# A two-path Mamba-2 stack with experts on one Trainium2 core: the next pass's constants and weight products taken later in a block, and the kernel's own constants built in four stages

## What is computed

```python
def mamba2(x, Win, conv_w, conv_b, dt_bias, A_log, D, gnorm, Wout):
    zxbcdt = x @ Win                                   # 64 -> 296
    z, xBC, dt = split(zxbcdt)                         # 128, 160, 8
    xBC = silu(conv_b + causal_conv4(xBC, conv_w))
    xs, B, C = split(xBC)                              # 128, 16, 16
    dt = softplus(dt + dt_bias)
    dA = exp(dt * -exp(A_log))
    # h_t = dA_t * h_{t-1} + xdt_t B_t ;  y_t = h_t C_t
    y = scan(dA, xs * dt, B, C) + D * xs
    return rmsnorm(y * silu(z), gnorm) @ Wout

for i in range(6):
    x = x + mamba2(rmsnorm(x, t_norm[i]), t_...[i])    # along time
    x = x + mamba2(rmsnorm(x, b_norm[i]), b_...[i])    # along bands
t = x_in + x
out = t + experts(layernorm(t))                        # 16 experts, top 2
```

## Time and profile before

| what | us |
|---|---|
| median of 3 runs | 1553.57 |
| lowest and highest run | 1553.42, 1564.56 |
| the profiled execution | 1553.12 |
| span of that execution | 1551.4 |
| busy: PE, DVE, ACT, POOL | 1220.9, 909.3, 720.8, 276.1 |

### The profile page before, as it was taken

One profiled execution on the slowest core, in us unless ns is written; L12 is line 12 of the kernel. 1 busy time (PEld: TensorE's weight loads), 2 busy tenths in 40 slices (PEclk: granted clock), 3 DMA queues, 4 the chain that ended last, 5 costly groups with the idle time before them and its releaser, 6 DMA issues. The chain is left out here.

```text
span 1551.4 us, 47280 instructions
## 1 busy us (share of the span) xinstructions
PE 1220.9 (79%) x20280; PEld 635.6 (41%) x20280; DVE 909.3 (59%) x1667; ACT 720.8 (46%) x1358; POOL 276.1 (18%) x406
## 2 busy tenths in 40 slices
PE   0688688688686886878868868778688962999998
PEld 0254344344343453434434434444344442333332
DVE  4276455565464565644745546546465576777776
ACT  1356455454364554645645536455456531333332
POOL 8011211221121112211212112112211151000000
PEclk8799899899898997998979979989899985999999
DMA  3010001100011000101001010001100022000000
GB/s 68 7 20 6 22 8 23 29 10 21 6 22 33 9 8 16 22 23 20 5 22 20 15 26 10 21 9 21 32 10 9 8 42 30 1 7 1 8 8 7
DMA packets 69600, 26.45 MB, mean 17 GB/s; under 512 B 54928, under 2 KB 66320, under 8 KB 69392
## 3 DMA queue, kind: packets, MB, share of 16 engines
q1 hardware_dynamic: 69392, 23.42, 7.5%
HBM read 9.96 MB, written 1.05 MB: 7 GB/s over the span
## 5 line engine op out<-in xcount | busy, mean ns | idle before, releaser
L1249 DVE TENSOR_TENSOR em<-em,gx 128x1536 f32<-128x1536 f32 (+1 forms) x192 | 283.7, 1478 | 134.4 <-ACT em L972 134.4
L972 ACT ACTIVATE em<-ring 128x512 f32<-128x512 f32 x480 | 255.1, 599 | 207.4 <-PE ring L725 207.2
L550 POOL TENSOR_TENSOR ysq<-yg 128x256 f32<-128x256 f32 x192 | 117.6, 612 | 900.5 <-DVE yg L1267 900.5
L725 PE MATMUL ring<-rt,lt 128*64 128x512 bf16 x960 | 152.9, 416 | 61.6 <-ACT em L972 45.5
L742 PE MATMUL ybank<-em,xdt 64*32 64x64 f32 (+1 forms) x12288 | 189.9, 244 | 0.9 <-issue 0.6
L742 PEld LDWEIGHTS ybank<-em,xdt 64*32 64x32 f32 x12288 | 157.6, 108 | 36.0 <-issue 35.2
L708 PE MATMUL gx<-cm,bc 16*64 16x128 f32 (+1 forms) x768 | 75.9, 275 | 81.8 <-DVE em L1249 79.7
L1105 ACT ACTIVATE em<-ring 128x512 f32<-128x512 f32 x128 | 69.5, 595 | 148.4 <-PE ring L862 148.4
L619 PE MATMUL ring<-xsq,mean 128*128 128x512 f32 x96 | 65.8, 775 | 89.9 <-ACT xsq L933 69.4
L991 ACT ACTIVATE xs<-ring,col 128x512 f32<-128x512 f32 x96 | 60.7, 683 | 147.8 <-PE ring L667 147.8
L1275 DVE TENSOR_TENSOR on<-oss,rr 128x256 f32<-128x256 f32 x96 | 40.2, 419 | 133.0 <-ACT rr L982 132.9
(11 more groups left out here) (168 smaller groups left out, 1692.4 us busy)
## 6 DMA issues: line engine op xcount, KB each, us to landing
x_b<-x_t SPq DMA_DIRECT2D x48, 128.0 KB, 3.0
rt<-lt SPq DMA_DIRECT2D x240, 12.0 KB
cm<-bc SPq DMA_DIRECT2D x96, 32.0 KB, 2.0
cw<-in_L_conv_t_cw SPq DMA_DIRECT2D x6, 320.0 KB
cw<-in_L_conv_b_cw SPq DMA_DIRECT2D x6, 320.0 KB
x_in<-in_x SPq DMA_DIRECT2D x4, 256.0 KB, 4.3
xs<-in_L_ffn_w SPq DMA_DIRECT2D x2, 512.0 KB, 7.1
zs<-in_L_ffn_w SPq DMA_DIRECT2D x2, 512.0 KB, 9.2
```

Of the source, the lines that this page charges most:

```text
L550: pool.tensor_tensor(out=ysq[u][:, i % 2, :], in0=yg[u][:, i % 2, :], in1=yg[u][:, i % 2, :], op=ALU.mult).then_inc(s_ysq, 1)
L725: mm = pe.matmul(o[HALF * ab:HALF * (ab + 1), :].rearrange("p (h t) -> p h t", h=HEADS), lt[:, n % 2, ab, i, :], rt[i // 4][:, blk, :, i % ...
L972: emptied(act.activation(em[:, p % EM_SLOTS, :, HALF * j:HALF * (j + 1)], o.rearrange("p (h t) -> p h t", h=HEADS), ACT.Exp), "seg", n, i, ...
L1249: dve.tensor_tensor(e, e, gx[:, 0:wide].rearrange("p (o t) -> p o t", o=1).to_broadcast([P, HEADS, wide]), ALU.mult).then_inc(s_w, 1)
```

## The change

It has three parts.

1. On ScalarE `exp_a(pass_of(k) + 1)` moves from between `exps(k, 2)` and `exps(k, 3)` to behind the silu burst and the table load that ends it.
2. On GpSimd `weights_made(pass_of(k) + 1)` moves from behind step `i == 1` to behind step `i == 6`, the seventh.
3. The constants are counted in four stages, `n_const[0]` to `[3]`: up to `ones64`; with `parts`; with `tok1h`, `rtmpl` and `rseq`; with `xdt`, `gate_w` and `rank`. `weights_made(0)` goes between the second and third, `weights_made(1)` behind the fourth. TensorE waits for stage 0 before the means, for stage 1 before `turn_parts(0)` and for `s_rep` 12 only before `decays(0, 0)`. VectorE fills `lt` behind `split_cum(0)`, and copies `rtmpl` into `rt` behind `rows_of_cum(0)`. SyncE's list is the same as before.

```diff
@@ gpsimd
             const(pool.memset(ones64[:], 1.0))
 
+            n_const[0] = made[0]
...
             for s in range(2):
                 const(pool.memset(parts[s][:], 0.0))
...
+            n_const[1] = made[0]
+            weights_made(0)
             const(pool.memset(tok1h[:], 0.0))
...
+            n_const[2] = made[0]
             for u in range(2):
                 const(pool.memset(xdt[u][:], 0.0))
             const(pool.memset(gate_w[:], 0.0))
             const(pool.iota(rank[:], pattern=[[-1, E]], base=E, channel_multiplier=0,
                             allow_small_or_imprecise_dtypes=True))
-            n_const[0] = made[0]
+            n_const[3] = made[0]
+            weights_made(1)
...
-            weights_made(0)
-            weights_made(1)
             for k in range(NBLOCK):
...
-                    if i == 1 and k % 2 == 0 and k >= 2 and pass_of(k) + 1 < NPASS:
+                    if i == 6 and k % 2 == 0 and k >= 2 and pass_of(k) + 1 < NPASS:
                         weights_made(pass_of(k) + 1)
@@ tensor
             pe.wait_ge(s_const, n_const[0])
-            pe.wait_ge(s_rep, 12)
             mean(0, 0)
...
             project_x(0, 1)
+            pe.wait_ge(s_const, n_const[1])
             turn_parts(0)
             project_z(0, 0)
             project_z(0, 1)
             g_and_xt(0, 0)
+            pe.wait_ge(s_rep, 12)
             decays(0, 0)
@@ scalar
                 exps(k, 2)
                 if k:
                     inverse_root(k - 1, 3)
-                if k % 2 == 0 and k >= 2 and pass_of(k) + 1 < NPASS:
-                    exp_a(pass_of(k) + 1)
                 exps(k, 3)
...
                     act.preload_act_table_set("natural_log_exp_and_others")
+                if k % 2 == 0 and k >= 2 and pass_of(k) + 1 < NPASS:
+                    exp_a(pass_of(k) + 1)
                 inverse_root(k, 2)
@@ vector
-            dve.wait_ge(s_const, n_const[0])
-            for u in range(2):
-                for i in range(4):
-                    dve.tensor_copy(rt[u]... , rtmpl...).then_inc(s_rep, 1)
-            for u in range(2):
-                dve.memset(lt[0:HALF, u], 0.0).then_inc(s_rep, 1)
-                dve.tensor_copy(lt[R_TOK:P, u]... , tok1h...).then_inc(s_rep, 1)
...
             finish_dt(0)
+            dve.wait_ge(s_const, n_const[1])
             split_cum(0)
+            dve.wait_ge(s_const, n_const[2])
+            for u in range(2):
+                dve.memset(lt[0:HALF, u], 0.0).then_inc(s_rep, 1)
+                dve.tensor_copy(lt[R_TOK:P, u]... , tok1h...).then_inc(s_rep, 1)
+            dve.wait_ge(s_rep, 4)
             rows_of_cum(0)
+            for u in range(2):
+                for i in range(4):
+                    dve.tensor_copy(rt[u]... , rtmpl...).then_inc(s_rep, 1)
+            dve.wait_ge(s_const, n_const[3])
             for k in range(NBLOCK):
```

More of the change, by code:

```diff
@@ L267, in build @@
         N_FIRST = 7
-        n_const = [0]
+        n_const = [0] * 4
         N_WLD = 22
@@ L543, in weights_made @@
                     [P, C]), op=ALU.mult).then_inc(s_wp, 1)
+            for s in range(2):
+                const(pool.memset(parts[s][:], 0.0))
+                for ab in range(2):
+                    rows = slice(HALF * ab, HALF * (ab + 1))
+                    const(pool.memset(parts[s][rows, :, R_TGT + NPART * ab:R_TGT + NPART * (ab + 1)], 1.0))
+            for ab in range(2):
+                v = parts[1][HALF * ab:HALF * (ab + 1), :, R_SEQ:R_SEQ + 4]
+                const(pool.memset(v, 1.0))
+                select(v, [[0, NPAIR], [-BANDS, 4]], 0, 1, ALU.is_ge, 0.0)
+                select(v, [[0, NPAIR], [BANDS, 4]], BANDS - 1, -1, ALU.is_ge, 0.0)
@@ new lines, in _ @@
+            n_const[1] = made[0]
+            weights_made(0)
+            const(pool.memset(tok1h[:], 0.0))
+            select(tok1h[R_TOK:P].rearrange("p (a t) -> p a t", a=2), [[0, 2], [-1, HALF]], 0, 1, ALU.not_equal, 1.0)
+            const(pool.memset(rtmpl[:], 0.0))
+            for r in range(NPART):
+                select(rtmpl[0:R_TGT, LL], [[-1, HEADS], [0, HALF]], -HEADS * r, 1, ALU.not_equal, -1.0)
+                select(rtmpl[0:R_TGT, LH], [[-1, HEADS], [0, HALF]], -HEADS * r, 1, ALU.not_equal, -1.0)
+                select(rtmpl[R_HIGH:R_HIGH + R_TGT, HH], [[-1, HEADS], [0, HALF]], -HEADS * r, 1, ALU.not_equal, -1.0)
@@ new lines, in _ @@
+            for blk in (LL, HH):
+                select(rtmpl[R_TOK:P, blk], [[0, HEADS], [1, HALF]], 0, -1, ALU.is_ge, FAR)
+            q0 = R_SEQ - R_HIGH
+            seqv = rseq[R_HIGH:R_TOK].rearrange("p h (q v) -> p h q v", q=4)
+            const(pool.memset(rseq[R_HIGH:R_TOK], FAR))
+            select(seqv, [[0, HEADS], [-1, 4], [0, BANDS]], -q0, 1, ALU.not_equal, 0.0)
+            select(seqv, [[0, HEADS], [0, 4], [0, BANDS]], -q0, 1, ALU.is_ge, 0.0)
+            select(seqv, [[0, HEADS], [0, 4], [0, BANDS]], q0 + 3, -1, ALU.is_ge, 0.0)
@@ new lines, in _ @@
+            for blk in (LL, HH):
+                const(pool.tensor_tensor(out=rtmpl[R_HIGH:R_TOK, blk], in0=rtmpl[R_HIGH:R_TOK, blk],
+                                         in1=rseq[R_HIGH:R_TOK], op=ALU.add))
+            n_const[2] = made[0]
+            for u in range(2):
+                const(pool.memset(xdt[u][:], 0.0))
+            const(pool.memset(gate_w[:], 0.0))
+            const(pool.iota(rank[:], pattern=[[-1, E]], base=E, channel_multiplier=0,
+                            allow_small_or_imprecise_dtypes=True))
@@ L1145, in _ @@
             from_banks(0, x_t)
-            dve.wait_ge(s_const, n_const[0])
-            for u in range(2):
-                for i in range(4):
-                    dve.tensor_copy(rt[u][:, :, :, i, :].rearrange("p b h t -> p (b h) t"),
-                                    rtmpl[:].rearrange("p b h t -> p (b h) t")).then_inc(s_rep, 1)
-            for u in range(2):
-                dve.memset(lt[0:HALF, u], 0.0).then_inc(s_rep, 1)
-                dve.tensor_copy(lt[R_TOK:P, u].rearrange("p a i t -> p (a i) t"), tok1h[R_TOK:P, 0:HALF].rearrange(
-                    "p (o t) -> p o t", o=1).to_broadcast([HALF, 2 * NPAIR, HALF])).then_inc(s_rep, 1)
             def filled(*key):
@@ L1280, in _ @@
             finish_dt(0)
+            dve.wait_ge(s_const, n_const[1])
             split_cum(0)
-            rows_of_cum(0)
+            dve.wait_ge(s_const, n_const[2])
+            for u in range(2):
+                dve.memset(lt[0:HALF, u], 0.0).then_inc(s_rep, 1)
+                dve.tensor_copy(lt[R_TOK:P, u].rearrange("p a i t -> p (a i) t"), tok1h[R_TOK:P, 0:HALF].rearrange(
+                    "p (o t) -> p o t", o=1).to_broadcast([HALF, 2 * NPAIR, HALF])).then_inc(s_rep, 1)
+            dve.wait_ge(s_rep, 4)
+            rows_of_cum(0)
+            for u in range(2):
+                for i in range(4):
+                    dve.tensor_copy(rt[u][:, :, :, i, :].rearrange("p b h t -> p (b h) t"),
+                                    rtmpl[:].rearrange("p b h t -> p (b h) t")).then_inc(s_rep, 1)
+            dve.wait_ge(s_const, n_const[3])
             for k in range(NBLOCK):
```

## The result

The changed kernel takes 1428.0 us (median of 4 runs, 1420.8 to 1429.3) against 1553.5 before in the same job: a ratio of 0.917, 95% interval 0.914 to 0.920. That is 125 us less, where 124.3 were forecast. The profiled execution took 1429.27, with a span of 1427.5.

A forecast was written before the change was run, and what follows sets the result against it. Bound by waits, no engine being full: mainly ScalarE's ten stalls for the `Alog` load. From 1553.1 us, 114.3 for the stalls (after 9.9 for clock dips) and 10 for the start gave 1428.8; range 1413 to 1447.

The forecast's parts named there:

- What bounds it, and the price of a stall: ScalarE's ten waits for the `Alog` load, 134.1 us in all, cost even blocks 124.2 us, 12.4 a pair.
- (1): ScalarE's `exp_a` behind the silu burst: the load is there some 20 us earlier, 0.21 us each as before, cost nothing.
- (2): GpSimd's weight products behind step 6: 2.92 us fits in 10.83 us of idleness, cost taken as 0.
- Rival C: Products at step 6 delay `add_x(k, 2)` and the next block's squares: 29 us more, 1458 us; chance 0.06.
- (3): Unstalled even blocks resemble their odd partners; three band and one time clock dips take 9.9 us, leaving a gain of 114.3.
- A: A clock dip in every freed block and the start at its lower bound: 1446 us; chance 0.14.
- F: No clock dip in any freed block: 1419 us; chance 0.16.
- B: Another wait replaces the removed one in the even blocks, half remains: 1481 us; chance 0.04.
- One sign that I gave: In the profile after, even and odd blocks of each pair were to be equal within 3 us.
- rival D: TensorE's clock falls and stays down through blocks 0 to 22, losing 410 us: 1839 us; chance 0.01.
- (4): At the start the first mean goes 19.0 us earlier, decays at 63.4 to 66.6; gain 10, bounds 5 and 13.

The follow-up runs named there:

- exp_step5: The changed kernel with `exp_a` ahead of `exps(k, 5)` instead of behind the silu burst: 1485.8 us, ratio 0.956.
- exp_only: The kernel before with only `exp_a` moved behind the silu burst; weight products stay behind step 1, start as before: 1493.6 us, ratio 0.958.
- no_start: The changed kernel with the start of the kernel before; `exp_a` and the later passes' products stay moved: 1438.9 us, ratio 0.925.
- products_x3: The changed kernel with the weight product `wt` done three times in each of the ten even blocks: 1422.7 us, ratio 0.916.
- start_only: The changed kernel with `exp_a` and the later passes' weight products back in their old places: 1545.8 us, ratio 0.992.
- early_rt: The changed kernel with the eight `rt` copies ahead of `rows_of_cum(0)` and SyncE's `c_rows(0)` ahead of its `s_rep` wait: 1416.6 us, repeated 1420.7.

## Why the prediction was right

**What bounds it, and the price of a stall.** Right. The difference of even and odd blocks gave 124.2 for ten stalls, and 119.9 went from the even blocks. exp_step5, with waits half as long, has a price near it: 1.05 us for each us of waiting against 0.89.

**(1) exp_a.** Right: no wait, 0.21 us ten times. exp_only shows a half that the prediction did not price. It took the two moves together and gave (2) a cost of 0 and no gain, as if the move of the products were only free. It is needed: left at step 1, the products cost some 55 us (exp_only's 1493.6 against no_start's 1438.9), once ScalarE's stall no longer hides them.

**(2) The products at step 6.** Right: 2.92 us in a gap that leaves 8.05. Rival C falls by products_x3.

**(3) What is late next.** The sum was right, 113.8 for 114.3, but not its parts, so that its closeness is luck. I subtracted 9.9 for dips in the freed blocks, three band and one time. They had one band dip and four time dips (blocks 8, 12, 16 and 20). Ten even blocks without a dip, at 42.36 and 47.42, would take 448.9, which is 126.7 less than the 575.6 before; the dips took back nearly all of 6.8, and the odd blocks, which I had left at their old time, another 6.1. I had priced a band dip at 2.75 by comparing block 22 with the odd band blocks (41.77). But an even band block without a dip lasts 42.36, and an even time block 47.42 where an odd one lasts 48.2: they are not quite like their odd partners. The dips cost 2.2 (for 2.75) and 1.0 to 1.2 (for 1.64). Rivals A and F bound it from both sides as they should. B has nothing in the changed kernel, as no wait came in place of the removed ones; exp_only is B's case, with GpSimd's wait in place of ScalarE's and half of the gain left.

One sign that I gave did not show: the pair 4 and 5 differs by 5.5 us (47.42 and 52.90), and not by less than 3, for the three dips in block 5. In rival D the clock would fall: it rose from 0.93 to 0.98 over blocks 2 to 21, and not to 1.00. (The rule that activity releases the throttle, of the Trainium skill's "TensorE: Matmul & The Clock Gate", "Part 1: The HAM clock gate (the "warmup" mystery)", fits the rise.)

The dips that remain come without a stall, but not without a wait. In block 10 the clock is 0.52 from 535 to 542, with TensorE busy 6.89 of the 7 us, and in the 7 us ahead, from 527 to 534 at a clock of 1.00, it was busy 4.46, with waits of 1.11 and 1.42 us. Block 22 before, which I called a block with no gap, has a wait of 1.42 us too, right ahead of its dip. Yet block 18 of the changed kernel was also busy 4.46 of the 7 us up to the same place, with the same two waits, and had no dip. So no row here tells which block dips. The rows of block 22 before (timeline of TensorE) and of block 10:

```profile
1203.33 0.33 PE L708 MATMUL gx<-cm,bc 16*64 16x64 f32 x4 [1.42 <-DVE em L1249]
```

```profile
535.00:542.00 7.00, 6.89 (x134) 2.97 (x115) 5.07 (x11) 2.69 (x5) 2.45 (x4) 0.52 0.27 60
```

**(4) The start.** 10 forecast, 10.2 measured, out of two errors that cancel. The chain was right step by step: weights at 17.7, mean at 25.08, rows of `lt` at 49.07, `cm` at 53.83. The copies took 3.84 and not 4.4, since they overlap by 0.08 each, and the decays began at 62.43, 1 us ahead of the early end: 12.8 gained where I took 11. Behind them 2.6 were lost (46.0 us from the decays to the table load for 43.4), at a clock of 0.87 for 0.97, where I took off 1. That the edit causes this loss is not shown. In the six profiles with the new start the decays began at 62.3 to 66.0 and these 46.0 us were 43.7 to 46.3; in the four with the old start it took 43.4 to 47.7. By the medians of start_only and no_start the start is worth 10 to 16 us. The replaced wait was the right one: early_rt takes it away and the decays come 5.5 to 6.6 us earlier.

## What to carry to other kernels

When two engines wait for the same load, the list of waits counts it twice. Here the shorter wait was worth nothing alone and over 50 us once the longer was gone: move both, and behind a stretch in which that engine is idle anyway. Where a kernel repeats a block with and without the suspect instruction, cutting the span at a mark that occurs once a block and taking the difference prices the stall better than its row does (here 124 us, where the row has 134 and 120 were gained). A job with time to spare at the head of an in-order queue was free here up to the idle time behind it, and the 5.5 us beyond it cost 6.2.

## What was not expected of the hardware

TensorE's granted clock falls to 1.2 GHz in blocks without any stall, nearly always at the same two places, in 7 us or 3 to 4 us pieces, and not in every block. Idle matmuls put into a pause raised the mean clock of a stretch from 0.50 to 0.90, and no gain can be seen in the time (1425.7 us for 1424.7). The copies of the earlier trace rows that took up to 1.88 us beside GpSimd's products take 0.55 alone, while the product beside them took up to 1.73 us for 1.54; a first product beside VectorE's `zs` took 2.67 us for 0.68. The share of both engines in the loss can be seen there, but no run here was made to split it.
